# A transformer block in fp32r parts: the high part of two tensors is written by ScalarE from PSUM, where GpSimd cast it from SBUF

## The chip, the cores and the metric

The kernel runs on one core of a Trainium2 chip. A core has TensorE (matmuls), VectorE, ScalarE, GpSimd and SyncE, which issues the DMAs here. The metric is the device time of one launch in microseconds. GpSimd does not touch the PSUM banks in this kernel.

## What is computed

A pre-norm block on 16 sequences of 512 tokens of width 256, fp32: attention with 16 heads of 16, then one linear layer on the values rounded to fp8.

```python
x = x + attn(layernorm(x))          # softmax(q k^T / 4) v, then the projection
y = layernorm(x)
y_q = clip(y / input_scale, -448, 448).astype(float8_e4m3fn).astype(f32) * input_scale
x = x + (y_q @ (weight_fp8 * weight_scale).T + bias)
```

## The kernel before

Each engine runs its own program, written out by hand, and the engines meet at semaphores only. The program of each is a loop of 18 slots; slot `u` of TensorE, ScalarE, VectorE and GpSimd does the first part of batch `u` (layer norm, transposes, q and k projections), the row maxima of batch `u-1`, the exponentials and values of batch `u-2`, and the output projection, second norm and linear layer of batch `u-3`. A slot has 32 steps. At every step TensorE issues two transposed score matmuls (line 457, `scores_t`, one for each half `g` of `ps_t`), two plain score matmuls for the maxima (line 471, `ps_s`), and at odd steps eight value matmuls (line 489). `scores_t` of step `s` and half `g` overwrites the bank that the exponential of step `s-1` and half `g` reads, so it waits for that one (`exp_done`); ScalarE's exponential (line 568) in turn waits for the matmul. All side work shares one bank, `ps_m`: the transposes of the normed input (line 355) stand at steps 12 and 14, the four q and k projections (line 371) at 16, 18, 20 and 22, and each waits until the bank's last reader has signalled.

Matmuls run on fp32r numbers, so a tensor is kept as a high part (rounded to fp32r) and a low part (the rest), and each product is taken in three terms. For the normed input, `copy_xnT` on ScalarE (line 587) copies the transposed half `c` from `ps_m` to `xnT`, GpSimd (`low_xnT`, line 905) casts it to the high part `xnT_p[:, 0]`, and subtracts that from `xnT` to the low part `xnT_p[:, 1]` (line 907). `xnT` is one buffer: ScalarE's copy of half 1 waits for the subtract of half 0 (`xnT_low`). Projection 0 waits for the subtract of half 1. For the results of the four projections, `copy_qk` on ScalarE (line 605) adds the bias and writes `parts[:, n, 1]`, GpSimd (`split`, line 928) casts it to `parts[:, n, 0]`, and subtracts in place (line 930); then SyncE stacks the parts by DMA into `qs` and `ks` (line 282), which the next slot reads. ScalarE's side operations stand behind the two exponentials of their step. Batch 0 is different in `before` too: there ScalarE writes both the high part and the whole (lines 584 and 604), and VectorE subtracts.

Of the kernel before, what the change touches and what calls it, by code (L numbers as in the profile page):

```python
# [7 lines left out]
F32R = mybir.dt.float32r  # L8
U32 = mybir.dt.uint32
ALU = mybir.AluOpType  # L10
ACT = mybir.ActivationFunctionType
# [49 lines left out]
def block_kernel(nc, x, qkv_wT, qk_bT, v_bT, proj_wT, proj_b, lin_wT, lin_b, in_scale, w_scale, eye, out):  # L61
# [4 lines left out]
    with ExitStack() as ctx:  # L66
        def sb(name, shape, dt=F32):
            return ctx.enter_context(nc.sbuf_tensor(name, shape, dt))

        def ps(name, shape):  # L70
            return ctx.enter_context(nc.psum_tensor(name, shape, F32))

        def sem(name):
            return ctx.enter_context(nc.semaphore(name))
# [24 lines left out]
        xnT = sb("xnT", [P, S])  # L99
        xnT_p = sb("xnT_p", [P, 2, NC, S], F32R)  # L100
        parts = sb("parts", [P, 2 * NT, 2, S])
# [35 lines left out]
        ps_t = ps("ps_t", [P, 2, S])  # L137
        ps_s = ps("ps_s", [P, 2, 2, S])
        ps_o = ps("ps_o", [P, S])
        ps_m = ps("ps_m", [P, S])  # L140
# [22 lines left out]
        v_done = sem("v_done")  # L163
# [31 lines left out]

        rs1_ready = sem("rs1_ready")
        xn_ready = sem("xn_ready")
        xnT_high = sem("xnT_high")
        xnT_low = sem("xnT_low")
        oT_low = sem("oT_low")  # L200
        high_ready = sem("high_ready")
        low_ready = sem("low_ready")
        res_ready = sem("res_ready")
        rs2_pow = sem("rs2_pow")
# [7 lines left out]
        def past(count):  # L212

            return not isinstance(count, int) or count > 0

        def run_slots(eng, slot, finish, prepare=None):

            def present(u):  # L220
                return lambda behind: 0 <= u - behind < B
            for u in range(NSLOT - 1):
                slot(u, u % 2, present(u))
                if u == 0 and prepare:
                    prepare()
            finish(B - 1)
# [332 lines left out]
        @block.scalar  # L559
        def _(act):  # L560
            def exps(b, s, a):
                n, w = s // 4, s % 4
                if w == 0 and a == 0 and past(UNITS * b + n - 1):
                    act.wait_ge(pv_done, UNITS * b + n - 1)
                if isinstance(b, int) and b == 0 and s == 0:
                    act.wait_ge(const_v, 9)
                act.wait_ge(st_done, 2 * (STEPS * b + s) + a + 1)
                nc.scalar.activation(pt[n % 2][:, w % 2 + 2 * a, w // 2, :], ps_t[:, a, :], ACT.Exp, scale=SCALE).then_inc(exp_done, 1)  # L568

            def copy_v(b, par, half):  # L570
                act.wait_ge(v_done, 2 * b + half + 1)
                if isinstance(b, int) and b == 0:
                    act.wait_ge(ones, 3)
                if past(UNITS * (b - 1)):
                    act.wait_ge(pv_done, UNITS * (b - 1))
                nc.scalar.copy(vt[par][:, 2 * half:2 * half + 2, :, 0:HD],  # L576
                               ps_m[:].rearrange("p (j h e) -> p j h e", j=2, h=H)).then_inc(v_ready, 1)

            def copy_xnT(b, c):

                bank = ps_t[:, c, :] if b == 0 else ps_m[:]
                act.wait_ge(xt_done, 2 * b + c + 1)
                if b == 0:
                    nc.scalar.copy(xnT_p[:, 0, c, :], bank)
                if past(2 * b + c):
                    act.wait_ge(xnT_low, 2 * b + c)
                nc.scalar.copy(xnT[:], bank).then_inc(xnT_ready, 1)  # L587

            def copy_oT(b, t):

                act.wait_ge(oT_ready, NT * b + t + 1)
                if past(b):
                    act.wait_ge(proj_done, 2 * b)
                nc.scalar.copy(oT_p[:, 0, t, :], oT[:]).then_inc(oT_high, 1)  # L594

            def copy_qk(b, par, n):

                t, bias = n // 2, b_qk[:, (n % 2) * NT + n // 2:(n % 2) * NT + n // 2 + 1]
                bank = ps_s[:, n // 2, n % 2, :] if isinstance(b, int) and b == 0 else ps_m[:]
                act.wait_ge(qk_done, 4 * b + n + 1)  # L600
                if past(b):
                    act.wait_ge(stacked[t][1 - par], 96 * (b - 2 + par) + 192)
                if b == 0:
                    nc.scalar.activation(parts[:, n, 0, :].bitcast(F32R), bank, ACT.Identity, bias=bias)
                nc.scalar.activation(parts[:, n, 1, :], bank, ACT.Identity, bias=bias).then_inc(whole_ready, 1)  # L605

            def copy_hqT(b):
                act.wait_ge(xq_done, b + 1)
                if past(b):
                    act.wait_ge(lin_done, 2 * b)  # L610
                nc.scalar.copy(hqT[:].rearrange("p c n -> p (c n)"), ps_m[:].bitcast(BF16)).then_inc(hqT_ready, 1)

            def slot(u, par, present):
                for s in range(STEPS):
                    if present(2):
                        exps(u - 2, s, 0)
                        exps(u - 2, s, 1)
                    if s == COPY_OT[1] and present(3):
                        copy_oT(u - 3, 1)
                    if s == COPY_OT[0] and present(2):  # L620
                        copy_oT(u - 2, 0)
                    if s in PROJECT_V and present(1):
                        copy_v(u - 1, 1 - par, PROJECT_V.index(s))
                    if s in TRANSPOSE_X and present(0):
                        copy_xnT(u, TRANSPOSE_X.index(s))
                    if s in PROJECT_QK and present(0):
                        copy_qk(u, par, PROJECT_QK.index(s))
                    if s == TRANSPOSE_HQ and present(3):
                        copy_hqT(u - 3)

            def finish(b):
                copy_oT(b, 1)
                for half in range(2):
                    act.wait_ge(xq_done, b + half + 1)
                    if half == 0:
                        act.wait_ge(lin_done, 2 * b)
                    nc.scalar.copy(hqT[:, :, 2 * half * P:2 * (half + 1) * P],
                                   ps_t[:, half, :].bitcast(BF16)[:, 0:S].rearrange("p (c n) -> p c n", c=NC)
                                   ).then_inc(hqT_ready, 1)


            act.wait_ge(half_set, 1)
            nc.scalar.activation(table[:], half_neg[:, 0:1], ACT.Exp)
            act.wait_ge(ident_in, 32)
            run_slots(act, slot, finish)
# [238 lines left out]
        def _(pool):  # L884
# [16 lines left out]
            def low_xnT(b, c):  # L901
                pool.wait_ge(xnT_ready, 2 * b + c + 1)
                if past(b):
                    pool.wait_ge(v_done, 2 * b)
                pool.tensor_copy(xnT_p[:, 0, c, :], xnT[:]).then_inc(xnT_high, 1)  # L905
                pool.wait_ge(xnT_high, 2 * (b - 1) + c + 1)
                pool.tensor_tensor(xnT_p[:, 1, c, :], xnT[:], xnT_p[:, 0, c, :].bitcast(F32),  # L907
                                   ALU.subtract).then_inc(xnT_low, 1)

# [15 lines left out]
            def split(b, n):  # L925

                pool.wait_ge(whole_ready, 4 * b + n + 1)
                pool.tensor_copy(parts[:, n, 0, :].bitcast(F32R), parts[:, n, 1, :]).then_inc(high_ready, 1)
                pool.wait_ge(high_ready, 4 * (b - 1) + n + 1)
                pool.tensor_tensor(parts[:, n, 1, :], parts[:, n, 1, :], parts[:, n, 0, :],  # L930
                                   ALU.subtract).then_inc(low_ready, 1)

# [41 lines left out]
            def slot(u, par, present):  # L974
# [6 lines left out]
                if present(0) and later:  # L981
                    low_xnT(u, 0)
                if present(2):
                    out_divide(u - 2, 0)
                if present(0) and later:
                    low_xnT(u, 1)
                if present(3):
                    layernorm_h(u - 3)
                if present(0) and later:
                    split(u, 0)  # L990
                    split(u, 1)
# [5 lines left out]
                if present(0) and later:  # L997
                    split(u, 2)
# [59 lines left out]
```

## Time and profile before

| | us |
|---|---|
| median of 3 runs (1048.88 to 1054.34) | 1050.12 |
| the profiled execution's own time | 1050.12 |
| its span in the profile | 1048.3 |
| TensorE busy | 945.9 (90%) |
| VectorE busy | 843.0 (80%) |
| ScalarE busy | 655.7 (63%) |
| GpSimd busy | 522.7 (50%) |

In the profile's rows PE is TensorE's matmul, PEld its weight load, DVE VectorE, ACT ScalarE, POOL GpSimd, SP SyncE. L457 is line 457 of the kernel. A release in square brackets names what ended the idle time before a row. The granted clock is a share of TensorE's full speed: 1.00 is 2.4 GHz, 0.50 is 1.2 GHz. A busy share is an average; whether an engine holds others up is read from the waits and the chain. The slots 3 to 15 all look alike, so that one of them, from about 527 to 585 us, stands for them.

### The profile page before, as it was taken

How to read it: one execution, taken by the hardware profiler on the slowest of the kernel's cores; microseconds unless marked ns; L12 is line 12 of the kernel's file. 1: busy time of each engine (PE TensorE's matmuls, PEld its weight loads, DVE VectorE, ACT ScalarE, POOL GpSimd, SP SyncE). 2: the span in 40 equal slices, each digit the busy share in tenths (PEclk: the TensorE clock that was granted, in tenths of full speed). 3: DMA queues.
4: the chain of work that ended last, by engine and by line, in shares of the span. 5: the costliest groups of instructions: out<-in, count | busy, mean ns of one | idle time of the engine just before them, and what ended most of it. 6: DMA issues, size and time to landing. Idle time of an engine off the chain costs nothing.

```text
span 1048.3 us, 16257 instructions
## 1 busy us (share of the span) xinstructions
PE 945.9 (90%) x5796; PEld 443.0 (42%) x5796; DVE 843.0 (80%) x1186; ACT 655.7 (63%) x1209; POOL 522.7 (50%) x533
## 2 busy tenths in 40 slices
PE   3476989999999999999999999999999999999884
PEld 2243334444444434454444444444444444433333
DVE  3586788888888989888888889888888888896226
ACT  3013776767676676767676676767676776766560
POOL 3141344828284654728293755638282846524242
PEclk9675999999999999999999999999999999999795
DMA  4928092656638192746648291836556380911010
GB/s 138 116 44 94 26 119 41 97 88 77 108 45 139 21 115 51 108 77 82 103 56 129 30 117 39 119 66 92 93 68 96 40 125 14 117 35 42 2 41 20
DMA packets 44289, 79.40 MB, mean 76 GB/s; under 512 B 9904, under 2 KB 13104, under 8 KB 44208
## 3 DMA queue, kind: packets, MB, share of 16 engines
q1 hardware_dynamic: 44208, 78.36, 50.5%
q8 instruction: 46, 0.75, 0.4%
q14 instruction: 35, 0.29, 0.1%
HBM read 18.42 MB, written 8.39 MB: 26 GB/s over the span
## 4 chain that ended last, share of the span: by engine, by line
PE 81%; ACT 6%; POOL 4%; DVE 3%; issue 2%; DMA 2%; SPq 1%; ACTq 0%; POOLq 0%; DVEq 0%
PE ps_t L457 28%; PE ps_o L489 23%; PE ps_m L371 9%; PE ps_s L471 5%; ACT pt L568 5%; PE ps_m L382 5%; PE ps_m L408 5%; PE ps_m L439 3%; POOL xnT_p L907 2%; SPq L282 1%; ACT xnT L587 1%; POOL xnT_p L905 1%; DVE mx L686 1%; DMA ks<-parts 1%; PE ps_m L355 1%
## 5 line engine op out<-in xcount | busy, mean ns | idle before, releaser
L568 ACT ACTIVATE pt<-ps_t 128x512 f32<-128x512 f32 x1024 | 557.5, 599 | 242.5 <-PE ps_t L457 238.0
L686 DVE TENSOR_REDUCE mx<-ps_s 128x2 f32<-128x1024 f32 x512 | 617.6, 1213 | 93.3 <-PE ps_s L471 87.9
L457 PE MATMUL ps_t<-qs,ks 50*128 50x512 f32 x1024 | 406.9, 467 | 41.1 <-ACT pt L568 34.7
L471 PE MATMUL ps_s<-ks,qs 48*128 48x512 f32 x1024 | 399.8, 472 | 20.0 <-DMA ks<-parts 11.4
L457 PEld LDWEIGHTS ps_t<-qs,ks 50*128 50x128 f32 x1024 | 164.7, 187 | 360.2 <-ACT pt L568 288.4
L489 PE MATMUL ps_o<-pt,vt 128*32 128x512 f32 x2048 | 275.3, 610 | 0.2 <-ACT pt L568 0.2
L471 PEld LDWEIGHTS ps_s<-ks,qs 48*128 48x128 f32 x1024 | 160.1, 189 | 31.3 <-DVE mx L686 16.1
L905 POOL CAST xnT_p<-xnT 128x512 fp32r<-128x512 f32 x30 | 18.3, 611 | 195.2 <-ACT xnT L587 195.2
L371 PE MATMUL ps_m<-xnT_p,wqkv_p 128*128 128x512 f32 x360 | 101.1, 417 | 7.6 <-POOL xnT_p L907 7.6
L939 POOL TENSOR_TENSOR on<-ot,rden 128x256 f32<-128x256 f32 x63 | 39.6, 628 | 103.8 <-DVE rden L745 103.8
L930 POOL TENSOR_TENSOR parts<-parts 128x512 f32<-128x512 f32 x60 | 81.2, 1353 | 4.9
L371 PEld LDWEIGHTS ps_m<-xnT_p,wqkv_p 128*128 128x128 f32 x360 | 64.0, 191 | 39.5 <-issue 27.2
L605 ACT ACTIVATE parts<-ps_m,b_qk 128x512 f32<-128x512 f32 x60 | 41.3, 688 | 57.9 <-PE ps_m L371 57.9
L914 POOL TENSOR_TENSOR oT_p<-oT,oT_p 128x512 fp32r<-128x512 f32 x31 | 39.8, 1283 | 72.6 <-ACT oT_p L594 72.6
L489 PEld LDWEIGHTS ps_o<-pt,vt 128*32 128x32 f32 x2048 | 40.6, 108 | 76.4 <-issue 71.8
L741 DVE STREAM_TRANSPOSE ot<-ps_o 128x512 f32<-128x512 f32 x64 | 45.2, 707 | 24.7 <-PE ps_o L489 24.7
L922 POOL TENSOR_TENSOR xres<-xres,b_proj 128x1024 f32<-128x1024 f32 x16 | 38.3, 2393 | 50.9 <-DMA xres<-in_x 50.9
L382 PE MATMUL ps_m<-wqkv_p,xnT_p 128*128 128x256 f32 x384 | 55.0, 294 | 0.0
L382 PEld LDWEIGHTS ps_m<-wqkv_p,xnT_p 128*128 128x128 f32 x384 | 48.6, 196 | 12.0 <-issue 11.6
L408 PE MATMUL ps_m<-wproj_p,oT_p 128*128 128x256 f32 x360 | 52.0, 295 | 0.0
L408 PEld LDWEIGHTS ps_m<-wproj_p,oT_p 128*128 128x128 f32 x360 | 45.8, 194 | 11.1 <-issue 11.1
L576 ACT COPY vt<-ps_m 128x512 f32<-128x512 f32 x32 | 18.8, 588 | 39.4 <-PE ps_m L382 39.4
(94 smaller groups left out, 766.4 us busy)
## 6 DMA issues: line engine op xcount, KB each, us to landing
qs<-parts SPq DMA_DIRECT2D x192, 128.0 KB, 6.5
ks<-parts SPq DMA_DIRECT2D x192, 128.0 KB, 7.0
xin<-in_x SPq DMA_DIRECT2D x16, 512.0 KB, 4.6
xres<-in_x SPq DMA_DIRECT2D x16, 512.0 KB, 5.9
out<-h SPq DMA_DIRECT2D x15, 512.0 KB, 9.0
qs<-nmax SPq DMA_DIRECT2D x128, 8.0 KB, 5.7
pt<-in_qkv_wT SPq DMA_DIRECT2D x1, 768.0 KB, 6.5
out<-h SPq DMA_DIRECT2D x2, 256.0 KB, 2.0
```

The costliest lines, as they stand in the source:

```text
L371: last = nc.tensor.matmul(bank, wqkv_p[:, pw, c, first:first + P], xnT_p[:, px, c, :], start=(m == 0 and c == 0), stop=(m == 2 and c == NC ...
L382: last = nc.tensor.matmul(ps_m[:, j * D:(j + 1) * D], xnT_p[:, px, c, tok], wqkv_p[:, pw, c, 2 * D:3 * D], start=(m == 0 and c == 0), stop ...
L408: last = nc.tensor.matmul(bank[:, j * D:(j + 1) * D], oT_p[:, px, t, tok], wproj_p[:, pw, t, :], start=(m == 0 and t == 0), stop=(m == 2 a ...
L457: nc.tensor.matmul(ps_t[:, g, :], ks[par][rows, slot, keys], qs[par][rows, slot, :], start=True, stop=True).then_inc(st_done, 1)
L471: done = nc.tensor.matmul(ps_s[:, s % 2, g, :], qs[par][rows, slot, queries], ks[par][rows, slot, :], start=True, stop=True)
L489: last = nc.tensor.matmul(ps_o[32 * i:32 * i + VW, :], vt[par][:, 2 * kp + a, head, :], pt[n % 2][:, i, a, :], start=(kp == 0 and a == 0), ...
L568: nc.scalar.activation(pt[n % 2][:, w % 2 + 2 * a, w // 2, :], ps_t[:, a, :], ACT.Exp, scale=SCALE).then_inc(exp_done, 1)
L605: nc.scalar.activation(parts[:, n, 1, :], bank, ACT.Identity, bias=bias).then_inc(whole_ready, 1)
L686: dve.tensor_reduce(mx[:, t, :, s % (STEPS // 2)], ps_s[:, s % 2, :, :], AX_X, ALU.max).then_inc(max_done, 1)
L741: dve.transpose(ot[:].rearrange("p a c -> p (a c)"), ps_o[:]).then_inc(ot_ready, 1)
L914: pool.tensor_tensor(oT_p[:, 1, t, :], oT[:], oT_p[:, 0, t, :].bitcast(F32), ALU.subtract).then_inc(oT_low, 1)
L930: pool.tensor_tensor(parts[:, n, 1, :], parts[:, n, 1, :], parts[:, n, 0, :], ALU.subtract).then_inc(low_ready, 1)
```

## The change

ScalarE writes the high part of both tensors from the bank, in every batch as it did in batch 0 before, ahead of the whole; GpSimd only subtracts. The wait for the values' projection of the batch before (`v_done`), which guards the overwriting of `xnT_p`, now stands on ScalarE as well. Two semaphores between GpSimd's cast and its subtract go.

```diff
--- before.py
+++ after.py
@@ -195,10 +195,8 @@
 
         rs1_ready = sem("rs1_ready")
         xn_ready = sem("xn_ready")
-        xnT_high = sem("xnT_high")
         xnT_low = sem("xnT_low")
         oT_low = sem("oT_low")
-        high_ready = sem("high_ready")
         low_ready = sem("low_ready")
         res_ready = sem("res_ready")
         rs2_pow = sem("rs2_pow")
@@ -578,10 +576,11 @@
 
             def copy_xnT(b, c):
 
-                bank = ps_t[:, c, :] if b == 0 else ps_m[:]
+                bank = ps_t[:, c, :] if isinstance(b, int) and b == 0 else ps_m[:]
                 act.wait_ge(xt_done, 2 * b + c + 1)
-                if b == 0:
-                    nc.scalar.copy(xnT_p[:, 0, c, :], bank)
+                if past(b):
+                    act.wait_ge(v_done, 2 * b)
+                nc.scalar.copy(xnT_p[:, 0, c, :], bank)
                 if past(2 * b + c):
                     act.wait_ge(xnT_low, 2 * b + c)
                 nc.scalar.copy(xnT[:], bank).then_inc(xnT_ready, 1)
@@ -600,8 +599,7 @@
                 act.wait_ge(qk_done, 4 * b + n + 1)
                 if past(b):
                     act.wait_ge(stacked[t][1 - par], 96 * (b - 2 + par) + 192)
-                if b == 0:
-                    nc.scalar.activation(parts[:, n, 0, :].bitcast(F32R), bank, ACT.Identity, bias=bias)
+                nc.scalar.activation(parts[:, n, 0, :].bitcast(F32R), bank, ACT.Identity, bias=bias)
                 nc.scalar.activation(parts[:, n, 1, :], bank, ACT.Identity, bias=bias).then_inc(whole_ready, 1)
 
             def copy_hqT(b):
@@ -902,8 +900,6 @@
                 pool.wait_ge(xnT_ready, 2 * b + c + 1)
                 if past(b):
                     pool.wait_ge(v_done, 2 * b)
-                pool.tensor_copy(xnT_p[:, 0, c, :], xnT[:]).then_inc(xnT_high, 1)
-                pool.wait_ge(xnT_high, 2 * (b - 1) + c + 1)
                 pool.tensor_tensor(xnT_p[:, 1, c, :], xnT[:], xnT_p[:, 0, c, :].bitcast(F32),
                                    ALU.subtract).then_inc(xnT_low, 1)
 
@@ -925,8 +921,6 @@
             def split(b, n):
 
                 pool.wait_ge(whole_ready, 4 * b + n + 1)
-                pool.tensor_copy(parts[:, n, 0, :].bitcast(F32R), parts[:, n, 1, :]).then_inc(high_ready, 1)
-                pool.wait_ge(high_ready, 4 * (b - 1) + n + 1)
                 pool.tensor_tensor(parts[:, n, 1, :], parts[:, n, 1, :], parts[:, n, 0, :],
                                    ALU.subtract).then_inc(low_ready, 1)
```

ScalarE's program in a slot, from the copy of the first transposed half at step 12 to the second projection's write at step 18 (`ps_t` holds transposed scores, `pt` their exponentials; the buffer numbers in the names of the semaphores change with the slot's parity). Before:

```order
L587 COPY xnT<-ps_m 128x512 [waits xnT_low,xt_done]
L568 ACTIVATE pt<-ps_t 128x512 [waits st_done] x4
L587 COPY xnT<-ps_m 128x512 [waits xnT_low,xt_done]
L568 ACTIVATE pt<-ps_t 128x512 [waits st_done] x2
L568 ACTIVATE pt<-ps_t 128x512 [waits st_done,pv_done]
L568 ACTIVATE pt<-ps_t 128x512 [waits st_done]
L605 ACTIVATE parts<-ps_m,b_qk 128x512 [waits stacked00,qk_done]
L568 ACTIVATE pt<-ps_t 128x512 [waits st_done] x4
L605 ACTIVATE parts<-ps_m,b_qk 128x512 [waits stacked00,qk_done]
L568 ACTIVATE pt<-ps_t 128x512 [waits st_done] x2
```

And now:

```order
L583 CAST xnT_p<-ps_m 128x512 [waits v_done,xt_done]
L586 COPY xnT<-ps_m 128x512 [waits xnT_low]
L566 ACTIVATE pt<-ps_t 128x512 [waits st_done] x4
L583 CAST xnT_p<-ps_m 128x512 [waits v_done,xt_done]
L586 COPY xnT<-ps_m 128x512 [waits xnT_low]
L566 ACTIVATE pt<-ps_t 128x512 [waits st_done] x2
L566 ACTIVATE pt<-ps_t 128x512 [waits st_done,pv_done]
L566 ACTIVATE pt<-ps_t 128x512 [waits st_done]
L602 ACTIVATE parts<-ps_m,b_qk 128x512 [waits stacked01,qk_done]
L603 ACTIVATE parts<-ps_m,b_qk 128x512
L566 ACTIVATE pt<-ps_t 128x512 [waits st_done] x4
```

Ahead of each copy into `xnT` and of each whole write of `parts` stands one more operation, and the exponentials behind it are moved back by it; the copy's wait for the subtract (`xnT_low`) is now behind the cast.

GpSimd's program at the transposed halves of one slot. Before:

```order
L905 CAST xnT_p<-xnT 128x512 [waits v_done,xnT_ready]
L907 TENSOR_TENSOR xnT_p<-xnT,xnT_p 128x512 [waits xnT_high]
L939 TENSOR_TENSOR on<-ot,rden 128x16x16 [waits oT_ready,rden_ready]
L905 CAST xnT_p<-xnT 128x512 [waits v_done,xnT_ready]
L907 TENSOR_TENSOR xnT_p<-xnT,xnT_p 128x512 [waits xnT_high]
```

And now:

```order
L903 TENSOR_TENSOR xnT_p<-xnT,xnT_p 128x512 [waits v_done,xnT_ready]
L933 TENSOR_TENSOR on<-ot,rden 128x16x16 [waits oT_ready,rden_ready]
L903 TENSOR_TENSOR xnT_p<-xnT,xnT_p 128x512 [waits v_done,xnT_ready]
```

At the first two projections, before:

```order
L928 CAST parts<-parts 128x512 [waits whole_ready]
L930 TENSOR_TENSOR parts<-parts 128x512 [waits high_ready]
L928 CAST parts<-parts 128x512 [waits whole_ready]
L930 TENSOR_TENSOR parts<-parts 128x512 [waits high_ready]
L939 TENSOR_TENSOR on<-ot,rden 128x16x16 [waits rden_ready]
```

And now:

```order
L924 TENSOR_TENSOR parts<-parts 128x512 [waits whole_ready] x2
L933 TENSOR_TENSOR on<-ot,rden 128x16x16 [waits rden_ready]
```

The casts are gone, six in a slot, and the subtracts wait for ScalarE's signals directly; the order of the rest is as it was.

## Rows read from the trace of the kernel before

**Rows 1.** The page: busy time of each engine, and the chain's shares by engine.

```profile
PE 945.9 (90%) x5796; PEld 443.0 (42%) x5796; DVE 843.0 (80%) x1186; ACT 655.7 (63%) x1209; POOL 522.7 (50%) x533
...
PE 81%; ACT 6%; POOL 4%; DVE 3%; issue 2%; DMA 2%; SPq 1%; ACTq 0%; POOLq 0%; DVEq 0%
```

**Rows 2.** Groups by line: busy us, mean ns of one, idle before.

```profile
L605 ACT ACTIVATE parts<-ps_m,b_qk 128x512 f32<-128x512 f32 x60 | 41.3, 688 | 57.9 <-PE ps_m L371 57.9
...
L928 POOL CAST parts<-parts 128x512 fp32r<-128x512 f32 x60 | 36.6, 610 | 11.7 <-ACT parts L605 11.7
```

**Rows 3.** Waits: us in total, times, longest us.

```profile
PEld ps_t L457 <- ACT pt L568: 288.4, 444, 1.3
...
PE ps_m L371 <- POOL xnT_p L907: 7.6, 15, 1.4
```

**Rows 4.** Windows: length; busy PE, PEld, DVE, ACT, POOL; clock; DMA share, GB/s.

```profile
60.00:75.00 15.00, 13.24 (x44) 7.27 (x44) 11.16 (x12) 3.33 (x5) 7.96 (x10) 0.74 0.11 23
...
526.00:585.00 59.00, 57.09 (x371) 26.49 (x370) 52.08 (x73) 41.20 (x78) 33.93 (x35) 1.00 0.56 82
```

**Rows 5.** Timeline of ScalarE in batch 0: start, length, instruction.

```profile
13.68 0.58 ACT L584 CAST xnT_p<-ps_t 128x512 fp32r<-128x512 f32 x1 [11.46 <-PE ps_t L355]
...
14.16 0.59 ACT L587 COPY xnT<-ps_t 128x512 f32<-128x512 f32 x1
...
19.84 0.69 ACT L604 ACTIVATE parts<-ps_s,b_qk 128x512 fp32r<-128x512 f32 x1 [3.75 <-PE ps_s L371]
...
20.42 0.68 ACT L605 ACTIVATE parts<-ps_s,b_qk 128x512 f32<-128x512 f32 x1
```

**Rows 6.** Timeline of ScalarE and TensorE around projection 1 of a slot.

```profile
530.04 0.69 ACT L605 ACTIVATE parts<-ps_m,b_qk 128x512 f32<-128x512 f32 x1 [1.17 <-PE ps_m L371]
...
530.62 1.07 ACT L568 ACTIVATE pt<-ps_t 128x512 f32<-128x512 f32 x2
...
531.94 0.39 PE L457 MATMUL ps_t<-qs,ks 50*128 50x512 f32 x1
...
532.25 1.67 PE L371 MATMUL ps_m<-xnT_p,wqkv_p 128*128 128x512 f32 x6
```

**Rows 7.** Timeline where TensorE waits for the second exponential.

```profile
524.63 1.08 ACT L568 ACTIVATE pt<-ps_t 128x512 f32<-128x512 f32 x2 [0.55 <-PE ps_t L457]
...
526.20 1.07 PE L489 MATMUL ps_o<-pt,vt 128*32 128x512 f32 x8
```

**Rows 8.** Timeline of both engines behind projection 3 of the slot.

```profile
542.39 1.07 ACT L568 ACTIVATE pt<-ps_t 128x512 f32<-128x512 f32 x2
...
543.36 0.50 PE L457 MATMUL ps_t<-qs,ks 50*128 50x512 f32 x1
...
543.95 1.09 ACT L568 ACTIVATE pt<-ps_t 128x512 f32<-128x512 f32 x2 [0.48 <-PE ps_t L457]
...
544.60 0.49 PE L457 MATMUL ps_t<-qs,ks 50*128 50x512 f32 x1 [0.50 <-ACT pt L568]
```

**Rows 9.** The chain ahead of projection 0, and the next slot's subtract.

```profile
525.60 0.60 ACT xnT L587
...
526.95 1.29 POOL xnT_p L907
...
528.37 1.63 PE ps_m L371 x6
...
585.28 1.29 POOL xnT_p L907
```

**Rows 10.** Batch 1: timeline of the second copy, then the chain.

```profile
60.31 0.58 ACT L587 COPY xnT<-ps_m 128x512 f32<-128x512 f32 x1 [2.12 <-POOL xnT_p L907]
...
63.06 2.90 PE ps_m L371 x6
...
69.10 0.70 ACT parts L605
...
70.54 1.29 POOL parts L930
```

## The prediction

> **What bounds the kernel now.** I read the page's busy line and chain first. TensorE is busy 945.9 of 1048.3 us and holds 81% of the chain that ended last; ScalarE has 6% of it and GpSimd 4% [rows 1]. Then the groups: ScalarE writes `parts` 60 times at 688 ns and GpSimd casts it 60 times at 610 ns [rows 2]; with 30 casts into `xnT_p` of the same 0.61 us these are what the change takes off GpSimd. Then the waits: TensorE's weight loads waited 444 times for a ScalarE exponential, 288.4 us in all (much of that overlaps matmuls still running), and GpSimd held TensorE up only 15 times, 7.6 us in all, of which the longest, 1.4, is batch 1's [rows 3]; the other 14 have 0.44 each. So GpSimd has nearly nothing to give back and ScalarE is the engine that TensorE looks to. Last the steady stretch: each slot takes 58.3 us (the same GpSimd subtract starts at 526.95 and, in the next slot, at 585.28) [rows 9], TensorE is busy for 57.09 of 59 us there at a granted clock of 1.00 [rows 4], and at every step it can issue a step's transposed scores only when the exponentials of the step before have left `ps_t`, a bank for each half. A delay of the second exponential is therefore a delay of all that TensorE has behind it.
>
> **What the change adds and removes.** In batches 1 to 15 ScalarE gets six more operations a batch, 90 in all, and GpSimd loses six. Batch 0 had both ScalarE writes already. The trace has the two forms there [rows 5]: the cast into `xnT_p` starts at 13.68 and the copy behind it at 14.16, so one more costs 0.48 us of ScalarE's queue; the two writes of `parts` start at 19.84 and 20.42, 0.58 us. (Their durations, 0.58 and 0.69, overlap the next operation.) ScalarE gains 15 x (2 x 0.59 + 4 x 0.69) = 59 us of busy time, GpSimd loses 90 x 0.61 = 55. Neither is the cost; what counts is what TensorE waits for. In batch 1 no exponentials run beside; in batches 2 to 15, 14 slots, they do.
>
> **Projections 0, 1 and 2 of a slot.** After projection 0 ScalarE writes `parts` at 530.04, then runs the next step's two exponentials from 530.62 for 1.07, to 531.69. TensorE's second transposed score of the following step starts at 531.94 and projection 1 at 532.25 [rows 6]. Nothing waits now; the slack of that score is 531.94 - 531.69 - 0.05 = 0.20 us. With the second write the exponentials end 0.58 later, at 532.27. Where TensorE does wait for the second exponential, what follows the scores starts 0.49 after its end: exponentials end at 524.63 + 1.08 = 525.71, the next work at 526.20 [rows 7]. So projection 1 starts at 532.27 + 0.49 = 532.76, 0.51 late. The next two projections stand the same way (the exponentials end at 535.62 and 539.54 and the projections start at 536.18 and 540.10, 0.56 after each). Three times 0.51 is 1.53 us. TensorE is in order, and what gets late (scores, the maxima on VectorE, the next values) only follows it. Bounds of one such step: from below the shortest spacing of a ScalarE write in the trace, 0.48, less the slack of 0.20, is 0.28; from above the write's whole 0.69 in place of 0.58, 0.62. I take 0.51, since the spacing is that of the very pair of operations.
>
> **Projection 3.** Its exponentials run from 542.39, and the next step's first score starts at 543.36, its exponential at 543.95, and TensorE waits for that one until 544.60 [rows 8]. With the added 0.58 the first exponential ends near 542.39 + 0.58 + 0.60 = 543.57, the score starts at 543.62, and a score with an empty queue reaches its exponential 0.53 later (0.49 for the score and 0.04, from 544.60 to 545.09 and on): 544.15 in place of 543.95. So 0.20 late. Bounds 0 and 0.51.
>
> **The transposes (steps 12 to 16).** The extra cast of half 0 makes the next exponentials 0.48 late, of which some 0.3 reaches TensorE and 0.1 is left a step on, since exponential and transposes overlap again. Half 1's cast then starts near 525.74 and the copy at 526.22, ending at 526.81, where before the copy ended at 526.20 and GpSimd's cast stood behind it [rows 9]. The subtract starts at 526.87 in place of 526.95, and ends at 528.15. TensorE's own scores would be through at 528.29 by the rule of the last two paragraphs, and projection 0 starts there, 0.08 earlier than the 528.37 of before: the wait of 0.44 us for GpSimd swallows ScalarE's delay. Bounds: all 0.44 gained, or 0.4 lost.
>
> **Sum.** A slot: 1.53 + 0.20 - 0.08 = 1.65 us; 14 slots: 23.1 us. Batch 1 gives something back, as nothing runs beside it and its chain goes through GpSimd [rows 10]. There the copy of half 1 waited 2.12 us for half 0's subtract, until 60.31, and TensorE started at 63.06. Now ScalarE's cast of half 1 stands in that wait, the copy starts near 60.35 and ends at 60.94, the subtract runs from 61.0 to 62.28, and TensorE starts at 62.42, 0.64 earlier. `parts` of projection 1: write at 69.10, subtract at 70.54 before; now 69.10 + 0.58 + 0.69 + 0.05 = 70.42, 0.12 earlier, and the SyncE transfers behind it with it. Minus 0.76. In all +22.3 us, on the profiled execution's 1050.12 us (span 1048.3 and 1.8 around it), which is also the median: 1072.4 us. All else on GpSimd gets earlier (its `hq`, and the subtracts ahead of the stack transfers, whose users come a slot later); no wait of TensorE in the steady slots names one of them, so I count nothing.
>
> **Occupancy.** The busy shares are 63% for ScalarE and 50% for GpSimd [rows 1]. Neither is the busiest, and yet 444 waits of TensorE name ScalarE [rows 3], so the shares don't price the move here. The Trainium skill (Perfetto Trace Analysis, Identifying the Most-Contended Engine) says to improve the engine with the highest occupancy first, and takes occupancy as a fair measure for these two; by that alone an exchange of 59 us on one for 55 on the other would cost nothing, the outcome of rival A. The Trainium skill (Perfetto Trace Analysis, Optimizing GPSIMD Operations) says to prefer other engines to GpSimd where possible, which would promise a gain, the outcome of rival B; the trace agrees as to the durations only (a subtract of 1.28 us on GpSimd, rows 9).
>
> **Rivals.**
> A: the exponentials' delay is hidden, because the pairs overlap more closely or TensorE's records show it later than it could run. For: no TensorE wait stands at the projections now. Against: slack is 0.20 us and the addition 0.48 to 0.58. Time: 1050.1 - 0.8 and up to +5 for steps at the low bound with the whole 0.44 gained (14 x (3 x 0.28 - 0.44) = 5.6): 1049 to 1055. Chance 8%: 6 within 0.5%, 2 slower by more.
> B, faster: the wait for GpSimd is the one that decides. Its place is projection 0; it saves 0.44 us in each of 14 slots and 0.76 in batch 1, if each exponential is less than 0.20 us late: 1050.1 - 6.2 - 0.8 = 1043 us. It decides from an added spacing below 0.20 us, under half of the smallest in the trace. Chance 3%.
> C: the clock. Before 90 us TensorE had waits of over a microsecond, and from 60 to 75 us the mean clock was 0.74 [rows 4]; the six matmuls of a projection took 2.90 us at 63.06 and 1.63 at 528.37 [rows 9, 10]. If the new gaps brought TensorE to its lower level (1.2 in place of 2.4 GHz) for the four projections of a slot: 14 x 4 x 1.27 = 71 us more, 1143. Against: waits of 0.5 us, several a slot, go with a clock of 1.00 now. Chance 3%.
> D: the change doesn't do what it says, both writes fall where ScalarE idles (1.17 us idle before the write at 530.04). It can't: that idle time is the wait for the projection itself, and the second write reads the same result. It has a part of A's chance.
>
> **How the numbers follow.** Forecast 86%: slower, 1072.4, its own range 1060 to 1081 (each step from 0.3 to 0.62). A 8, B 3, C 3. The range that holds 8 in 10: 1060 to 1081. A measurement of this kernel tells 0.5%, about 5 us, from no change. Slower 0.86 + 0.02 + 0.03 = 0.91, same 0.06, faster 0.03.
>
> **What would show it.** In the profile after: ScalarE near 715 us busy, GpSimd near 468; a slot of about 60.0 us; two writes 0.58 apart after each projection; small TensorE waits for exponentials ahead of projections 1 to 3, some 0.3 us each; the wait of projection 0 for GpSimd down from 0.44 to nearly nothing, and TensorE there at 62.4 in batch 1; a clock of 1.00 in the slots. It would be wrong if the slot stayed at 58.3, if the wait showed up in VectorE's maxima, or if projection 0 was itself late by over 0.3 us.

## The result and the profile after

The changed kernel took 1082.18 us in the median of 4 runs (1075.93 to 1088.58), the kernel before 1049.5 (1048.65 to 1054.34) beside it: a ratio of 1.030, with an interval of 1.023 to 1.037. Forecast were 1072.4 us and a range of 1060 to 1081, so the direction was right and the time lies outside the range: 32 us were lost, where 22 were forecast. The profiled execution took 1080.5 us, its span is 1078.7.

| | before | after |
|---|---|---|
| ScalarE busy, us | 655.7 | 707.2 |
| GpSimd busy, us | 522.7 | 465.6 |
| projection 0 of batch 1 starts at, us | 63.06 | 62.66 |
| projection 0 of batch 2 | 120.72 | 120.88 |
| projection 0 of batch 15 | 878.42 | 908.95 |
| from there to the end of the span | 169.9 | 169.7 |

So the whole loss that shows lies between batches 2 and 15, in 13 slots: 30.4 us. The slot of batch 15 has its part of the delay too (from its projection 0 to its projection 3 it takes 11.76 us before and 13.24 after), but the stretch from there to the end also depends on TensorE's clock: over the profiles of all the kernels here, batch 15's projection 0 is followed by 165.5 us (the kernel of run 7, mean clock 0.93) to 178.4 us (the kernel of run 2, mean clock 0.84). A term of 1.7 us can't be read there.

These are lines of the page after, which answer to [rows 1]; in the second, each digit is TensorE's granted clock in a fortieth of the span, in tenths (9 is 90% or more):

```profile
PE 975.6 (90%) x5796; PEld 451.3 (42%) x5796; DVE 857.8 (80%) x1186; ACT 707.2 (66%) x1299; POOL 465.6 (43%) x443
...
PEclk9666999999998999999999999999999999999966
...
PE 74%; ACT 14%; DVE 6%; issue 2%; DMA 2%; SPq 1%; POOL 1%; ACTq 0%; DVEq 0%; POOLq 0%
```

ScalarE's share of the chain went from 6% to 14%, VectorE's from 3% to 6%, GpSimd's from 4% to 1%. The digit 8 in the thirteenth place of the clock's row is in a slot that took 65 us. The waits after, which answer to [rows 3] (us in total, times, longest):

```profile
PEld ps_t L455 <- ACT pt L566: 307.2, 474, 1.6
...
PE ps_t L455 <- ACT pt L566: 39.1, 120, 0.8
...
PE ps_s L469 <- DVE mx L684: 12.1, 23, 1.1
...
PE ps_s L469 <- DMA ks<-parts: 11.6, 1, 11.6
```

TensorE's wait for GpSimd is gone from the slots, as forecast; its weight loads wait for the exponentials more often (474 times in place of 444). What was not forecast is that TensorE waits for VectorE's maxima in four of the steady slots (those of batches 4, 5, 6 and 14). Before it did so in none of them; all of the total before lies ahead of batch 2's projection 0:

```profile
PE ps_s L471 <- DVE mx L686: 8.6, 16, 1.1
```

The distances from one projection 0 to the next, read from the timelines of TensorE, are all 58.3 to 58.4 us before (57.43 for the slot of batch 2). After, and with the duration of VectorE's `nm` operation in the same slot (a `tensor_scalar` on 128x4 numbers, line 702 before and 700 after, the end of the next batch's first norm):

```
slot of batch      2     3     4     5     6     7     8     9    10    11    12    13    14
distance, us   59.37 60.12 61.06 64.97 60.67 60.17 60.10 60.35 60.08 60.07 60.07 60.06 60.98
nm, us          1.55  1.08  2.11  2.07  1.77  1.27  0.91  0.94  0.94  1.02  1.12  0.92  2.08
```

Two things are in these rows. (The 60.35 of batch 9 belongs to neither: TensorE waits there for an exponential for 0.78 us, where the longest such wait of its neighbours is 0.51, and run 1 has the same.) The slot is about 60.07 us at its shortest, 1.74 more than before. And where `nm` takes more than about 1.3 us, the slot is longer still, by 0.6 to 1.0 us and once by 4.9 (0.26 for the slot of batch 2).

**The forecast part.** Timeline of ScalarE and TensorE around projection 1 of a steady slot of the changed kernel, which answers to [rows 6]:

```profile
549.01 0.69 ACT L602 ACTIVATE parts<-ps_m,b_qk 128x512 fp32r<-128x512 f32 x1 [0.89 <-PE ps_m L369]
...
549.60 0.68 ACT L603 ACTIVATE parts<-ps_m,b_qk 128x512 f32<-128x512 f32 x1
...
550.16 2.27 ACT L566 ACTIVATE pt<-ps_t 128x512 f32<-128x512 f32 x4
...
550.81 0.50 PE L455 MATMUL ps_t<-qs,ks 50*128 50x512 f32 x1 [0.19 <-ACT pt L566]
...
551.73 1.66 PE L369 MATMUL ps_m<-xnT_p,wqkv_p 128*128 128x512 f32 x6
```

Two writes of `parts` 0.59 us apart, the exponentials behind them, TensorE waiting 0.19 us for the first of those until 550.81, and projection 1 at 551.73. From projection 0 (547.34) to projection 3 (560.57) it is 13.23 us, where it was 11.73 before (528.37 to 540.10).

**The collision.** `nm` before and after; columns are the number of operations, then the shortest, median and longest duration in ns. Before:

```profile
L702 DVE TENSOR_SCALAR nm<-mv x16: 170/170/171, 6.3 to 846.0; 128x4 f32<-128x4 f32 x16
```

After, with the same operation of the second norm (line 718) for comparison:

```profile
L700 DVE TENSOR_SCALAR nm<-mv x16: 170/1054/2108, 6.3 to 875.6; 128x4 f32<-128x4 f32 x16
...
L718 DVE TENSOR_SCALAR nm<-mv x15: 170/170/172, 177.3 to 1016.4; 128x4 f32<-128x4 f32 x15
```

The slot of 65 us, timeline of the changed kernel:

```profile
328.74 2.40 POOL L918 TENSOR_TENSOR xres<-xres,b_proj 128x1024 f32<-128x1024 f32 x1 [2.12 <-DMA xres<-in_x]
...
329.10 2.07 DVE L700 TENSOR_SCALAR nm<-mv 128x4 f32<-128x4 f32 x1
...
331.16 1.21 DVE L684 TENSOR_REDUCE mx<-ps_s 128x2 f32<-128x1024 f32 x1
...
332.52 0.50 PE L469 MATMUL ps_s<-ks,qs 48*128 48x512 f32 x2 [0.21 <-DVE mx L684]
...
334.21 0.63 PE L469 MATMUL ps_s<-ks,qs 48*128 48x512 f32 x2 [0.66 <-DVE mx L684]
```

GpSimd starts its addition to `xres` (the bias of the output projection) at 328.74 for 2.40 us; `nm` starts at 329.10 and ends within 0.03 us of the addition's end, at 331.17, after 2.07 us in place of 0.17. The maxima start at 331.16, and TensorE waits for them twice. Before, `nm` was through 0.5 us ahead of the addition (the slot of batch 9):

```profile
554.30 0.17 DVE L702 TENSOR_SCALAR nm<-mv 128x4 f32<-128x4 f32 x1
...
554.96 2.41 POOL L922 TENSOR_TENSOR xres<-xres,b_proj 128x1024 f32<-128x1024 f32 x1 [3.14 <-DMA xres<-in_x]
```

And TensorE's clock behind it (windows of the changed kernel: length, busy of PE, PEld, DVE, ACT and POOL, clock, DMA share, GB/s):

```profile
328.00:332.00 4.00, 4.00 (x29) 1.94 (x25) 3.97 (x8) 2.48 (x5) 3.08 (x2) 1.00 0.00 1
...
332.00:336.00 4.00, 3.13 (x12) 1.00 (x15) 3.96 (x5) 2.28 (x4) 2.50 (x5) 0.80 0.92 138
...
336.00:340.00 4.00, 3.74 (x20) 1.27 (x16) 1.90 (x3) 1.72 (x4) 0.00 (x0) 0.50 1.08 115
...
344.00:348.00 4.00, 3.99 (x26) 2.10 (x26) 1.80 (x5) 1.87 (x4) 0.00 (x0) 0.92 0.75 163
```

After the two waits the clock is at 0.50, its lower level of 1.2 GHz, until about 344 us. The slot's 4.9 us are 0.87 of these waits and some 4.0 of the lower clock. The waits alone don't tell whether the clock falls: in the slot of batch 4 they were longer, the clock stayed at 1.00, and the slot is 0.99 us over, which is the two waits added up (0.27 and 0.73):

```profile
271.50 0.51 PE L469 MATMUL ps_s<-ks,qs 48*128 48x512 f32 x2 [0.27 <-DVE mx L684]
...
273.20 0.51 PE L469 MATMUL ps_s<-ks,qs 48*128 48x512 f32 x2 [0.73 <-DVE mx L684]
```

Why do they meet now? The reload of `xres` is issued by SyncE 20.7 us after projection 0 before and 22.5 us after it now, in step with the longer slot. The issues before and after (SPq is SyncE's DMA queue):

```profile
549.09 0.51 SPq L269 DMA_DIRECT2D xres<-in_x  x1
```

```profile
569.80 0.51 SPq L267 DMA_DIRECT2D xres<-in_x  x1
```

But it lands sooner, by the pages' medians of the time from issue to landing (the last column), before and after:

```profile
xres<-in_x SPq DMA_DIRECT2D x16, 512.0 KB, 5.9
```

```profile
xres<-in_x SPq DMA_DIRECT2D x16, 512.0 KB, 3.8
```

So in the slot of batch 9 GpSimd's addition starts 26.2 us behind projection 0 in place of 26.6 (over the slots of batches 3 to 14: 26.15 to 27.35 in place of 26.59 to 27.96), while `nm` starts at 27.7 in place of 25.9, for the slot was stretched by 1.7 ahead of it. That the landing is quicker because the stacked transfers ahead of it are through by then was not tested.

### The profile page after: what moved, and what is told of

It is laid out like the page before. It is cut to its first block, busy times and chain, and to the rows that moved or that the text cites. A ratio compares the mean times of both kernels' runs of the same rounds, so it can differ in the third digit from the quotient of the medians.

```text
span 1078.7 us, 16257 instructions
## 1 busy us (share of the span) xinstructions
PE 975.6 (90%) x5796; PEld 451.3 (42%) x5796; DVE 857.8 (80%) x1186; ACT 707.2 (66%) x1299; POOL 465.6 (43%) x443
## 4 chain that ended last, share of the span: by engine, by line
PE 74%; ACT 14%; DVE 6%; issue 2%; DMA 2%; SPq 1%; POOL 1%; ACTq 0%; DVEq 0%; POOLq 0%
PE ps_t L455 27%; PE ps_o L487 18%; PE ps_m L369 9%; ACT pt L566 6%; PE ps_m L380 5%; PE ps_m L406 4%; PE ps_s L469 4%; ACT parts L602 4%; ACT parts L603 3%; DVE mx L684 3%; PE ps_m L437 2%; PE ps_m L353 2%; DMA ks<-parts 1%; PE ps_m L420 1%; DVE nm L700 1%
## 5 line engine op out<-in xcount | busy, mean ns | idle before, releaser
L455 PE MATMUL ps_t<-qs,ks 50*128 50x512 f32 x1024 | 424.4, 474 | 44.3 <-ACT pt L566 39.1
L469 PE MATMUL ps_s<-ks,qs 48*128 48x512 f32 x1024 | 413.1, 482 | 23.6 <-DVE mx L684 12.1
L455 PEld LDWEIGHTS ps_t<-qs,ks 50*128 50x128 f32 x1024 | 168.5, 187 | 386.1 <-ACT pt L566 307.2
L469 PEld LDWEIGHTS ps_s<-ks,qs 48*128 48x128 f32 x1024 | 162.8, 190 | 37.6 <-DVE mx L684 19.4
L903 POOL TENSOR_TENSOR xnT_p<-xnT,xnT_p 128x512 fp32r<-128x512 f32 x30 | 38.3, 1277 | 212.7 <-ACT xnT L586 212.7
L924 POOL TENSOR_TENSOR parts<-parts 128x512 f32<-128x512 f32 x60 | 76.6, 1277 | 37.4 <-ACT parts L603 37.4
L602 ACT ACTIVATE parts<-ps_m,b_qk 128x512 fp32r<-128x512 f32 x60 | 41.3, 688 | 65.5 <-PE ps_m L369 65.5
```

What stands on the lines that cost most here:

```text
L455: nc.tensor.matmul(ps_t[:, g, :], ks[par][rows, slot, keys], qs[par][rows, slot, :], start=True, stop=True).then_inc(st_done, 1)
L469: done = nc.tensor.matmul(ps_s[:, s % 2, g, :], qs[par][rows, slot, queries], ks[par][rows, slot, :], start=True, stop=True)
```

## The experiments

All ratios are to the kernel before on the same chip. Times of different runs are compared by their ratios, since the kernel before itself had 1051.5 to 1054.1 us beside them.

**1. The addition kept apart from `nm`.** The changed kernel with one wait more:

```diff
                     out_divide(u - 2, 2)
+                    if present(-1):
+                        pool.wait_ge(ln1_ready, 2 * (u + 1) + 2)
                     add_bias(u - 2)
```

> The changed kernel, but GpSimd waits for VectorE's small norm operations (ln1_ready of the next batch) before it adds the bias to xres, so that the two do not run side by side. Theory K (collision): in the changed kernel VectorE's nm operation (16 of them) takes 1.05 us in the median and up to 2.11, where it took 0.17 before, because it starts while GpSimd's 2.4 us addition to xres runs; where it takes over about 1.1 us, the maxima get late, TensorE waits, and in one slot its clock fell. Then here nm takes 0.17 in every slot, every steady slot takes 60.1 us, no slot has a clock below 1.00, and the time is 1050 + 14 x 1.74 = 1074 us, with little spread between runs. Rival G (the gaps ahead of the projections let the clock fall by themselves): nm is short, but slots of 61 to 65 us remain and the time stays at 1080 with runs 10 us apart.

Measured: 1076.84 us, ratio 1.021 (1.019 to 1.023). Eleven slots of 60.05 to 60.07 and 60.41 us once (the slot of batch 2 has 59.11), `nm` at 0.17 everywhere, and the clock at 1.00 in all these slots. The window over them and the row of `nm`:

```profile
118.00:900.00 782.00, 753.47 (x4694) 345.75 (x4691) 667.88 (x932) 572.10 (x1056) 375.82 (x356) 1.00 0.53 79
...
L700 DVE TENSOR_SCALAR nm<-mv x16: 170/170/171, 6.3 to 866.8; 128x4 f32<-128x4 f32 x16
```

The ratio of 1.0213 on 1049.5 us is 1071.9 us (1069.8 to 1074.0), which holds the forecast's own 1072.4. The gaps ahead of the projections are all still there, and the clock is 1.00 throughout the window: rival G (that the gaps ahead of the projections lower the clock) falls, and what the forecast lacked is the collision. The runs still spread over 6.5 us (1073.57 to 1080.11), so the little spread that was expected did not come. It does not lie in the slots, which agree to 0.03 us but for one; in this profile the stretch behind batch 15's projection 0 takes 177.5 us, in place of 169.9.

**2. Only `parts`.** `copy_qk` and `split` as in the change, `copy_xnT` and `low_xnT` as before.

> Only the half of the change that concerns parts: ScalarE writes their high part, GpSimd only subtracts; xnT_p as in the kernel before. By the forecast's terms (three projections 0.49 late, 0.2 to 0.28 behind the fourth) a slot is 1.7 us longer, nothing comes from xnT_p, and the time is 1074, or up to 1082 if VectorE's nm operation and GpSimd's addition collide here too. If the transposes' part carried some of the 1.74 us, the slot would be 59.5 us or less here and the time under 1067.

Measured: 1090.62 us, ratio 1.032 (1.029 to 1.036). Steady slots from 60.08 us, `nm` at 0.89 to 2.06 us, and two slots of 63.22 and 63.54. All of the slot's loss comes from `parts`. By the ratio the time is 1083.5 us on 1049.5, a little above the expected 1082. In this profile the clock fell in two slots and not in one, but the interval holds the whole change's 1.030 and 1.031, so a costlier collision is not shown.

**3. Only `xnT_p`,** the other half, run twice.

> Only the half of the change that concerns xnT_p: ScalarE writes its high part, GpSimd only subtracts; parts as before. Forecast's term: minus 0.08 us a slot and minus 0.64 in batch 1, so 1048 us, no change that a measurement tells. Rival: the added cast holds the exponentials up by 0.48 us twice a slot and TensorE pays for one of them: plus 0.3 to 0.5 a slot, 1054 to 1057. Rival B of the prediction in its purest form would be 1043.

Measured: 1051.57 us, ratio 0.997 (0.995 to 1.000), steady slots of 58.26 to 58.35 us, `nm` 0.17. Most are 58.27, minus 0.06 a slot, where the forecast had minus 0.08.

> The xnT half of the change once more, beside the two others: a slot of 58.27 us in its profile and a ratio of 0.997 in the first set. Forecast's term says minus 0.08 us a slot and 0.64 in batch 1, minus 1.8 us in all, 0.998; if the first result was chance, 1.000 with an interval over both signs.

Measured: 1053.9 us, ratio 0.999 (0.997 to 1.001), slots of 58.27 to 58.35. A gain that small is not shown by the time; the slot shows it.

**4. ScalarE's work added, GpSimd's kept.** The change's edits in `copy_xnT` and `copy_qk`; GpSimd still casts, over the same values.

> ScalarE's six operations a batch are added as in the change, GpSimd keeps its casts (the high parts are written twice with the same values). If the loss is all ScalarE's, it is at least as large here as with the change: 1.75 us a slot from the projections, and projection 0 about 0.5 later, since GpSimd's cast still stands ahead of its subtract: 14 x 2.25 = 31, 1081 us. If instead the loss came from GpSimd running earlier (its additions colliding with VectorE's operations), the kernel would be near 1050 here, with nm at 0.17 us.

Measured: 1094.91 us, ratio 1.038 (1.036 to 1.040). The slots without a collision (`nm` 0.17) have 60.72 to 60.74 us, 2.40 more than before; those with `nm` at 1.67 to 2.35 have 61.3 and over (60.78 for batch 2's slot), and one 65.96. The time is above the expected 1081 (1089 by the ratio): the slot's 2.25 was nearly right, but no collision was counted, and ten slots have one. The loss is ScalarE's, and with GpSimd's casts in place it is larger, so these were worth 0.66 us a slot once ScalarE did the work. The collision also came with GpSimd no lighter: the stretched slot is enough to bring it about. (Run 9 shows that it is not the only way.)

**5. The change again.**

> The changed kernel as it is, beside the other kernels of this set and against the kernel before on their chip. Both theories: a ratio of about 1.030. With the kernel in which GpSimd's addition waits for VectorE at 1.021, theory K (collision of VectorE's nm operation with GpSimd's addition to xres, and the fall of TensorE's clock that may follow) owes about 0.9% here: nm at 0.9 to 2.1 us, a slot of 60.1 where it is under about 1.3 us, of 60.5 to 65 where it is over. If the ratio is 1.021 here too, the difference between the two was the chip's and K is worth nothing.

Measured: 1084.41 us, ratio 1.031 (1.027 to 1.035), with four slots of 60.91 to 61.09 us and one of 63.24, all at `nm` over 1.7. Against 1.021 with the two kept apart, the collision and what follows is worth 1.0% of the time, some 10 us; the two intervals do not touch.

**6. The collision alone, in the kernel before.** VectorE's norm numbers wait for the landing on which GpSimd's addition waits:

```diff
                         if s == LN1_END:
+                            if present(2):
+                                dve.wait_ge(xr_in, 16 * (u - 2) + 16)
                             ln1_finish(u + 1)
```

> The kernel before, in which VectorE starts its norm operations of the next batch only when the reload of xres has landed, so that they meet GpSimd's addition; nothing is changed on ScalarE or in the casts. Theory K: nm takes about 2.0 us in place of 0.17 in the 14 slots that have both, the maxima behind it get late by 2.7 us in all, TensorE waits for them about 1 us a slot (59.3), and in some slots its clock falls for another 3 to 5 us: 1065 to 1085. Rival G (it needs ScalarE's gaps to lose time): the slot stays within 0.3 us of 58.33 and the time at or below 1055.

Measured: 1127.70 us, ratio 1.073 (1.070 to 1.076). Slots of 63 to 65 us (59.06 for batch 2's). The window over the steady slots, then `nm` and TensorE's wait for the maxima:

```profile
180.00:955.00 775.00, 729.00 (x4352) 335.48 (x4348) 640.98 (x865) 488.10 (x902) 403.17 (x410) 0.92 0.51 74
```

```profile
L702 DVE TENSOR_SCALAR nm<-mv x16: 170/1900/1927, 6.2 to 918.0; 128x4 f32<-128x4 f32 x16
...
PE ps_s L471 <- DVE mx L686: 41.7, 42, 2.3
```

No cast and no ScalarE operation was touched, and 76 us are gone; the clock is at 0.92 in the mean, where it was 1.00 in these slots before. Rival G's 1055 is far off. So is the expected 1065 to 1085: the clock fell in 12 of the 13 slots, not in some, and TensorE waited for the maxima for 1.7 to 3.2 us a slot, not about 1.

**7. Its control:** the same wait, and GpSimd's addition behind `nm` (the edits of 1 and 6).

> Control for the run before it: VectorE waits for the same landing, but GpSimd's addition waits for VectorE, so that they do not run side by side. VectorE is then late by only the 0.7 us between its old place and the landing. Theory K: nm 0.17 us, slots of 58.3 to 58.5 us, clock 1.00, time within 0.4% of the kernel before. If the loss is due to the wait for the landing and not to the collision, this kernel is as slow as the other.

Measured: 1065.33 us, ratio 1.013 (1.009 to 1.017). The same rows:

```profile
180.00:890.00 710.00, 684.57 (x4339) 319.37 (x4339) 613.80 (x861) 487.03 (x900) 400.33 (x407) 0.99 0.55 81
```

```profile
L702 DVE TENSOR_SCALAR nm<-mv x16: 170/170/171, 6.3 to 858.5; 128x4 f32<-128x4 f32 x16
...
PE ps_s L471 <- DVE mx L686: 14.1, 26, 1.1
```

So 6% of the time, in run 6, is the collision with the fall of the clock behind it, at the same wait for the landing. But the wait alone cost 1.3%, not under 0.4% as expected. VectorE stood idle for the landing for 1.04 to 2.16 us in each slot of batches 3 to 14, not for 0.7, and that already made slots of 58.5 to 59.7 us and one of 63.5. The profile is of the shortest execution (1057.35 us); what the others of up to 1070.44 lost more was not traced.

**8. The second write moved back a step.** In the changed kernel `copy_qk` writes only the high part behind the exponentials of its step, and the whole behind those of the next:

```diff
                     if s in PROJECT_QK and present(0):
                         copy_qk(u, par, PROJECT_QK.index(s))
+                    if s - 1 in PROJECT_QK and present(0) and u > 0:
+                        copy_qk(u, par, PROJECT_QK.index(s - 1), True)
```

> The changed kernel, with ScalarE's second write of parts (the whole) moved behind the exponentials of the following step; the high part stays where it was. If the slot's loss is the delay of the exponentials that TensorE waits for at once (forecast's term), it goes nearly away: TensorE's next projection waits about 0.1 us for the bank three times, and the slot is 58.3 + 0.3 - 0.1 = 58.5 us; nm is back at 0.17 since the slot is no longer stretched; time 1050 to 1054 against 1049.5. If ScalarE's added busy time of 2.76 us a slot costs wherever it stands, the slot stays at 60 us and the time above 1070.

Measured: 1056.58 us, ratio 1.0035 (1.001 to 1.006), which is 1053.2 us on 1049.5, as expected; slots of 58.56 us, `nm` 0.17. Timeline around a projection 1 of this kernel:

```profile
532.64 0.69 ACT L603 ACTIVATE parts<-ps_m,b_qk 128x512 fp32r<-128x512 f32 x1 [0.88 <-PE ps_m L369]
...
533.23 1.07 ACT L566 ACTIVATE pt<-ps_t 128x512 f32<-128x512 f32 x2
...
534.18 0.70 ACT L605 ACTIVATE parts<-ps_m,b_qk 128x512 f32<-128x512 f32 x1
...
534.93 1.67 PE L369 MATMUL ps_m<-xnT_p,wqkv_p 128*128 128x512 f32 x6
```

The exponentials at 533.23 follow the first write without a second before them, and projection 1 starts 3.97 us behind projection 0 (4.39 in the changed kernel). The same added operations of ScalarE cost 0.23 us a slot in place of 1.74 where the second write stands behind the exponentials that TensorE waits for at once. It was the place, not the amount.

**9. GpSimd lighter, ScalarE untouched.** The casts write 8 of 512 columns; the high parts keep old values otherwise.

```diff
-                pool.tensor_copy(parts[:, n, 0, :].bitcast(F32R), parts[:, n, 1, :]).then_inc(high_ready, 1)
+                pool.tensor_copy(parts[:, n, 0, 0:8].bitcast(F32R), parts[:, n, 1, 0:8]).then_inc(high_ready, 1)
```

> The kernel before, in which GpSimd's six casts a batch write 8 of the 512 columns (the rest of the high parts is left out and keeps old values), so that GpSimd loses nearly the same time as with the change, and ScalarE gains none. It prices what lighter GpSimd work is worth at most. Rival B's figure: TensorE's wait of 0.44 us for GpSimd's subtract goes in 14 slots, and some 0.6 to 1.2 us in batch 1: a slot of 57.9 us, 1050 - 7 = 1043 us, ratio 0.993. If nothing waits for GpSimd, 1050. If lighter GpSimd work by itself makes its addition to xres meet VectorE's nm operation, the time is above 1055 with nm over 1 us.

Measured: 1057.3 us, ratio 1.003 (1.000 to 1.005). Most slots have 57.93 to 57.99 us, rival B's figure, but three collided, 59.2, 63.1 and 59.2 us:

```profile
L702 DVE TENSOR_SCALAR nm<-mv x16: 169/170/2419, 6.3 to 847.6; 128x4 f32<-128x4 f32 x16
```

Both expectations came true in one kernel, and the time of neither: ten slots gain some 0.4 us each, and the three collisions lose 7.6. Here the slot is not stretched; the reload of `xres` lands up to 0.7 us sooner than before, and the addition starts up to 0.7 us earlier. The kernel before has 0.5 us between `nm` and the addition, and that is not enough.

**10. One subtract on VectorE.** The kernel before, with half 1's subtract of `xnT_p` taken by VectorE behind the maxima of step 14:

```diff
+                    if s == TRANSPOSE_X[1] and present(0) and u > 0:
+                        dve.wait_ge(xnT_high, 2 * (u - 1) + 2)
+                        dve.tensor_tensor(xnT_p[:, 1, 1, :], xnT[:], xnT_p[:, 0, 1, :].bitcast(F32),
+                                          ALU.subtract).then_inc(xnT_low, 1)
```

> The kernel before, in which VectorE, not GpSimd, takes the subtract of half 1 of xnT (0.69 us there, as in batch 0, where GpSimd needs 1.28), right behind the maxima of step 14; ScalarE and parts are untouched. TensorE's 0.44 us wait for that subtract is on the chain and VectorE is free near 526.9 in the slot, so the slot should be 57.9 us and the time 1043, ratio 0.993. If VectorE's maxima are delayed by it so that TensorE waits for them, the slot is 58.3 or more, ratio 1.000 to 1.005.

Measured: 1044.02 us, ratio 0.990 (0.987 to 0.992), slots of 57.86 to 57.93 us, as expected (56.95 for batch 2's). This kernel is faster than both. Its slots account for some 6 us of the 11 that the ratio gives, where 7 were expected; the rest was not traced. Timeline of the piece:

```profile
522.75 0.61 POOL L909 CAST xnT_p<-xnT 128x512 fp32r<-128x512 f32 x1 [0.54 <-ACT xnT L587]
...
523.39 0.69 DVE L808 TENSOR_TENSOR xnT_p<-xnT,xnT_p 128x512 fp32r<-128x512 f32 x1
...
524.35 1.66 PE L371 MATMUL ps_m<-xnT_p,wqkv_p 128*128 128x512 f32 x6
```

The cast ends at 523.36, the subtract takes 0.69 us, and TensorE's projection 0 starts at 524.35 with no wait before it, in place of 0.44 us.

## Why the prediction was wrong, step by step

- **Projections 0 to 2**, forecast 3 x 0.51 = 1.53 us a slot: 13.23 less 11.73 is 1.50. Right, mechanism and size.
- **Projection 3 and the transposes**, forecast 0.20 and minus 0.08: the rest of the steady slot (from projection 3 to the next projection 0) went from 46.61 to 46.84 us, 0.23 in place of 0.12. With only `parts` changed (run 2) it is 46.83, so projection 3 is 0.22, about as forecast. The transposes are minus 0.06 by themselves (slots of 58.27 with only `xnT_p` changed, against 58.33), but beside the changed `parts` only minus 0.01 is left of them (60.07 and 60.08).
- **The slot**, forecast 1.65: 1.74 where nothing collides. Run 1 gives the sum, with 1071.9 us. That it meets 1072.4 to 0.5 us is in part luck, since the interval is 2 us to either side: 13 slots lost 22.2 us to what was forecast, where 13 times 1.65 is 21.5, and neither the fourteenth slot nor batch 1's 0.76 can be seen in the traces.
- **Batch 1**, forecast minus 0.76 us: projection 0 came 0.40 earlier. Counted from the transposes of half 0 (56.52 before, 56.73 after) it is 6.54 and 5.93 us, 0.61 earlier where 0.64 was forecast; the other 0.21 was lost ahead of them. But then projections 0 to 2 ran at the lower clock, 2.9 us each, where in [rows 10] the first did. The chain's rows after:

```profile
62.66 2.91 PE ps_m L369 x6
...
66.91 2.94 PE ps_m L369 x6
...
71.19 2.94 PE ps_m L369 x6
...
75.47 1.67 PE ps_m L369 x6
```

  By projection 0 of batch 2 nothing was left of it (plus 0.16). The clock of this stretch differs between executions (projection 0 of batch 2 starts at 119.0 us in run 1 and at 121.7 in run 5, the changed kernel again), and the forecast had a single one.
- **What failed** are the two sentences that priced the rest at nothing: that what gets late, the maxima on VectorE among it, "only follows", and that of all else on GpSimd "no wait of TensorE in the steady slots names one of them, so I count nothing". The stretched slot moved VectorE's `nm` by 1.7 us, past the start of GpSimd's addition to `xres`, from which it had been 0.66 us away (554.30 and 554.96), and the two engines do not run these two side by side. The 13 distances exceed 60.07 us (59.11 for batch 2's slot, as in run 1) by 0.26, 0.05, 0.99, 4.90, 0.60, 0.10, 0.03, 0.28, 0.01, 0, 0, 0 and 0.91, 8.1 us in all. Of these 0.28 are batch 9's exponential, some 4.0 the clock's in one slot, and the rest, 3.8, is the collision's own delay. That is what lay between 1072 and 1080.5. The prediction had named the sign, among what would show it wrong: "if the wait showed up in VectorE's maxima".
- **The range** ended at 1081, because its upper end was built from the bounds of the projections alone. The failed term was not among its bounds. The other signs came: GpSimd 465.6 us busy (forecast 468), the slot, the two writes 0.59 apart; ScalarE has 707.2, forecast 715.
- **Rival C** (the clock, 3%) was half right: the clock did fall, not from the new gaps ahead of the projections (1.00 in run 1, with all of them), but behind waits for VectorE that the collision made. **Rivals A, B and D** fell; B's mechanism is real, and run 10 shows it when nothing else moves: 0.47 us a slot.
- The busy shares were set against the waits, and the waits were the better guide: the same operations on an engine 63% busy cost 1.74 us a slot at one place and 0.23 at another. The rule of the Trainium skill (Perfetto Trace Analysis, Identifying the Most-Contended Engine), to optimize the engine with the highest occupancy first, has no term for the place and would have priced both alike.

## What to carry to other kernels

When a slot is stretched on one engine, list the pairs of operations on VectorE and GpSimd that stand within a few microseconds of each other, and ask which pass each other: a pair with 0.6 us between them is a term of the sum. Move an operation to an engine that is waited for only behind the work that is waited for, not ahead of it. And price a late VectorE not by its delay alone: the clock may fall behind the wait, which cost 4.0 us here where the delay cost 0.9.

## What the runs showed of the hardware

A `tensor_scalar` of VectorE on 128x4 numbers in SBUF, 0.17 us, took up to 2.42 us (run 9) when it started within a GpSimd `tensor_tensor` of 2.4 us, and ended within 0.03 us of it. Beside the same addition of the changed kernel a `tensor_reduce` from PSUM (at 936.69, the addition from 936.25 to 938.65) took 1.23 us, and four `bn_aggr` (VectorE's means and variances, at 574.61 to 574.83, the addition from 573.53 to 575.92) 0.14 to 0.17 each, both as usual. This is the rule of the Trainium skill (SBUF — State Buffer, Who interferes with whom): the pair of SBUF ports that VectorE and GpSimd share is an exclusive lock, a `tensor_scalar` can take it, the one that comes second is blocked until the other's instruction ends, and a `tensor_reduce` never contends. The trace agrees, with 2.07 us at 329.10; the forecast had not asked for it.

The clock of TensorE fell to 0.50 behind waits for VectorE of 0.21 and 0.66 us, 1.7 us apart, while in run 1 seven waits of over 0.15 us for ScalarE in nearly every slot, 1.95 us together, left it at 1.00. It did not fall in every collided slot, and the length of the waits for the maxima does not say where: it fell with 0.33 us of them in the slot of batch 5 of run 2, and not with 1.70 in batch 2's of run 6. In four of the kernels the slot of batch 5 fell (64.97, 63.22, 65.96 and 63.51 us), each time between 328 and 339 us. What sets it apart is left open.
